# Two tiles of L1 scores move from VectorE to ScalarE and TensorE, and the scores' rows change order so that four transfers a pair spread them

## The chip, the cores and the metric

One NeuronCore of a Trainium2 chip runs the whole kernel in one launch. The metric is device time in microseconds; the other cores are idle. TensorE (matmuls into the eight PSUM banks), VectorE, ScalarE and GpSimd each run a hand-written stream of instructions, SyncE (SP) issues the transfers, and semaphores are the only order between them.

## The reference, cut to what matters

A small vision tower: a wavelet tokenizer, linear attention, a mixture of experts, then **L1-distance attention**, then a routed MLP. 128 images of 64 tokens, 64 features, 8 heads. Only the L1 attention is touched:

```python
q, vf, vb = v[:, :, :h], v[:, :, h:2*h], v[:, :, 2*h:]      # v = x @ wqv.T + b
k = x[:, :, None, :] * wk
a[b, s, t, h] = -sum_w |q[b, s, h, w] - k[b, t, h, w]| / 8   # w = 64 wide
a = softmax over s (with one extra zero row)
o = sum over heads of (a @ vf + a^T @ vb);  y = gelu-like(o) @ fanin;  x + y
```

So for every image there are 64 x 64 token pairs x 8 heads, each a sum of 64 absolute differences.

## The kernel before

Images go in pairs (`PAIRS` = 64), and the scores of each image in 16 tiles of 1024 columns. A tile is a difference q - k of 128 rows (token pairs) x 16 x 64: TensorE makes it by float16 matmuls that pick rows of q and k (high and low halves) out of `blocks`, two matmuls of 512 columns a tile. What is then done with it is set by `ORDER`, a string of 16 letters:

- **D** (11 of 16 before): VectorE reduces the absolute values straight from PSUM into `score` (`reduce`). There are two pairs of banks (0-1 and 2-3), so TensorE may be two D tiles ahead; it waits on `X["red"]` (in `image`).
- **A** (5 of 16): ScalarE takes the absolute values of banks 4 and 5, one bank at a time, into `absd` (`absolute`); GpSimd adds them up by a tree of halvings (`batch`).

The loop over pairs (`pair` on each engine) is unrolled for four pairs and then runs two pairs a turn. Between the tiles TensorE does the small work of the next and the last pairs, at positions written out by hand: in `pair` the inner function `extra(b, k)` is called after tile k of image b. Image 0 carries the next pair's turn, `queries`, `low(…, 0)` and `keys`, and the last pair's values; image 1 carries `low(…, 1)` and, for the pair before the last, `turn_attn` and the three parts of `attend`. Banks 6 and 7 serve these. `low` computes the low halves of q and k: it makes the float32 product again and takes the float16 high half from it with `neg_eye`.

When a pair's scores are complete, SP spreads them (`spread`): eight transfers an image, from 32 rows each, into `attn`, where ScalarE takes the exponentials in two parts of four heads (`exponentials`). GpSimd normalises (`normalise`). Pair q - 1's spreads and exponentials run during pair q, its attend steps during pair q + 1. SP issues, in order: `fill_blocks` for image 1, the spreads, `fill_blocks` for the next pair's image 0, and the load of a pair.

Of the kernel before, what the change touches and what calls it, by code (L numbers as in the profile page):

```python
# [36 lines left out]
ORDER = "DADDADDADDADDADD"  # L37
ND, NA = ORDER.count("D"), ORDER.count("A")
# [36 lines left out]
def constants():  # L75
# [9 lines left out]
    pick = np.zeros((4, 32, 8, 4, 32))  # L85
    for g in range(8):
        for x in range(4):
            for y in range(32):
                pick[0, 8 * x + g, g, x, y] = 1.0
                pick[1, 8 * x + g, g, x, y] = 1.0 / LO_SCALE  # L90
                pick[2, y, g, x, y] = -1.0
                pick[3, y, g, x, y] = -1.0 / LO_SCALE

    both = np.zeros((2, 32, 8, 2, 64))
    for e in range(EXPERTS):
        both[0, e, e // 2, e % 2] = 1.0
        both[1, e, e // 2, e % 2] = 1.0 / LO_SCALE
    same_head = np.kron(np.eye(16), np.ones((8, 8)))
# [5 lines left out]
        "c_both": both.reshape(64, 8 * P).astype(np.float16),  # L104
        "c_head": same_head.astype(np.float32),
# [5 lines left out]
def build(nc, a, out, scratch):  # L111

    with ExitStack() as ctx:
# [3 lines left out]
        def sem(name):  # L117
# [13 lines left out]
        c_cols = sb("c_cols_sb", [7, 2, 8, P])  # L131
# [15 lines left out]
        absd0 = sb("absd0", [P, NA * 1024])  # L147
        kT = absd0[:, 2048:3072].rearrange("p (b a m) -> p b a m", b=2, a=4)
# [35 lines left out]
        neg_eye = sb("neg_eye", [P, P], F16)  # L184
        xs1 = sb("xs1", [P, 2 * D])
# [60 lines left out]
        absd = [t[:].rearrange("p (n w) -> p n w", w=D) for t in (absd0, absd1)]  # L246
# [20 lines left out]
            "diffD", "diffA", "red", "abs", "tree", "pooled", "spread0", "spread1", "exp", "zr", "attk", "attq_ps", "attq",  # L267
# [92 lines left out]
        L1_IN = 16 * 5  # L360
        GATE = 14
        MLP_IN = 16 * 6
        PADS = 19
# [4 lines left out]
        def _(sp):  # L368
# [32 lines left out]
            sp.dma_start(rank[:], a["c_rank"]).then_inc(moe_in, 16)  # L401
            sp.dma_start(both[:].rearrange("p a b -> p (a b)"), a["c_both"]).then_inc(moe_in, 16)
# [48 lines left out]
            def pair(q, odd, at, following):  # L451
                fill_blocks(q, 1, at == 0)
                if at >= 1:
                    spread(q - 1, 1 - odd, 0, at == 1)
                    spread(q - 1, 1 - odd, 1, at == 1)
# [11 lines left out]
            spread(PAIRS - 1, 1, 0, False)  # L467
            spread(PAIRS - 1, 1, 1, False)
            sp.wait_ge(X["tb0"], 16 * 8 * (PAIRS + 1))
# [9 lines left out]
        def _(pe):  # L479
# [220 lines left out]
            def turn(p, at):  # L700

                if at >= 3:
                    pe.wait_ge(X["sum"], p - 3)
                pe.wait_ge(X["xs"], 16 * (p + 1))
                pe.transpose(ps[7][:, 0:P], xs1[:], ident[:]).then_inc(X["xT_ps"], 1)
# [43 lines left out]
            def attend(p, odd, part):  # L749

                if part == 0:
                    pe.wait_ge(X["attq"], p + 1)
# [25 lines left out]

            def image(q, b, at, extra):
# [3 lines left out]
                pe.wait_ge(X[f"tb{b}"], 16 * 8 * (q + 1))  # L783
                for k, path in enumerate(ORDER):
                    if path == "D":
                        if not (at == 0 and b == 0 and d < 2):
                            pe.wait_ge(X["red"], ND * s + d - 1)
                        unit, bank, done = 2 * d, 2 * ((b + d) % 2), "diffD"
                        d += 1
                    else:  # L790

                        for n in range(2):
                            if not (at == 0 and b == 0 and u == 0):
                                pe.wait_ge(X["abs"], 2 * NA * s + 2 * u + n - 1)
                            unit = 2 * (ND + u) + n
                            pe.matmul(ps[4 + n], pick[:, unit % 8, :], blocks[:, b, unit // 16, unit // 8 % 2, :],  # L796
                                      start=True, stop=True).then_inc(X["diffA"], 1)
# [9 lines left out]
            def pair(q, odd, at):  # L807
                def extra(b, k):
                    if b == 0:
# [16 lines left out]
                    else:  # L826
                        if k == 0:
                            low(q + 1, 1 - odd, 1)
                        if at >= 2:
                            if k == 4:  # L830
# [21 lines left out]
            fan_in(last - 2)  # L852

# [74 lines left out]
        def _(act):  # L928
            act.dma_start(c_cols[:].rearrange("p a b c -> p (a b c)"), a["c_cols"]).then_inc(tok_in, 16)
# [113 lines left out]
            def high_q(p, first):  # L1043
                act.wait_ge(X["q_ps"], p + 1)
                if not first:
                    act.wait_ge(X["tb0"], 16 * 8 * p)
                    act.wait_ge(X["tb1"], 16 * 8 * p)
# [20 lines left out]
            def absolute(s, odd, u, first):  # L1068

                for n in range(2):  # L1070
                    act.wait_ge(X["diffA"], 2 * NA * s + 2 * u + n + 1)
                    if u == 0 and n == 0 and not first:
                        act.wait_ge(X["pooled"], s - 1)
                    nc.scalar.activation(absd[odd][:, 16 * u + 8 * n:16 * u + 8 * n + 8, :],  # L1074
                                         ps[4 + n].rearrange("p (h w) -> p h w", w=D), ACT.Abs).then_inc(X["abs"], 1)

            def exponentials(p, part, first):

                if part == 0:
                    act.wait_ge(X["spread0"], 16 * 8 * (p + 1))  # L1080
# [561 lines left out]
```

## Time and profile before

| | us |
|---|---|
| median of 3 runs | 2579.07 (2578.93 to 2579.52) |
| the profiled execution | 2576.05 |
| its span, first to last instruction | 2574.2 |
| TensorE busy | 2236.6 (87%) |
| VectorE busy | 2244.8 (87%) |
| GpSimd busy | 1767.2 (69%) |
| ScalarE busy | 1475.2 (57%) |

The span is that of one execution taken by the hardware profiler. Matmuls are pipelined and their ends are modelled, so on TensorE the distance from start to start says more than the length of a record. A float32 matmul leaves two records. The L1 attention lies between about 720 and 2465 us of the span.

### The profile page before, as it was taken

What the parts mean: (1) busy time and instruction counts of PE and PEld (TensorE: products, weight loads), DVE (VectorE), ACT (ScalarE), POOL (GpSimd) and SP (SyncE); (2) the same over time, 40 slices, a digit from 0 to 9 for tenths busy, and PEclk for the clock granted to TensorE, in tenths of its full rate; (3) what the DMA queues carried; (4) which work ended last, traced back from release to release, by engine and by line L of the source; (5) the groups of instructions that cost most, each with busy time, mean ns of one, the idle gap of its engine ahead of it and who ended that gap; (6) DMA issues with size and microseconds to landing.
All of it is one profiled execution on the core that took longest, in us unless ns stands there. A gap on an engine that the chain in (4) does not pass through costs nothing.

```text
span 2574.2 us, 45353 instructions
## 1 busy us (share of the span) xinstructions
PE 2236.6 (87%) x12251; PEld 961.1 (37%) x12251; DVE 2244.8 (87%) x2638; ACT 1475.2 (57%) x3772; POOL 1767.2 (69%) x1033
## 2 busy tenths in 40 slices
PE   5558999999388989989989989899899899899878
PEld 3443333333123333333333333333333333333347
DVE  3877777777879999999999999999999999999974
ACT  0325555555146666666666666666666666666656
POOL 0112333333459889888888988888898888889843
PEclk8788999999689999999999999999999999999979
DMA  5200000000012112121211221221221212212201
GB/s 132 65 1 1 1 0 0 0 0 0 3 47 52 48 48 52 48 50 49 51 48 48 52 50 45 51 51 45 50 52 48 50 48 50 50 47 52 50 19 32
DMA packets 163216, 102.06 MB, mean 40 GB/s; under 512 B 55773, under 2 KB 161182, under 8 KB 163039
## 3 DMA queue, kind: packets, MB, share of 16 engines
q1 hardware_dynamic: 162858, 101.41, 16.0%
q8 instruction: 21, 0.34, 0.1%
q10 hardware_dynamic: 316, 0.12, 0.0%
q14 instruction: 21, 0.17, 0.0%
HBM read 10.63 MB, written 4.19 MB: 6 GB/s over the span
## 4 chain that ended last, share of the span: by engine, by line
PE 65%; DVE 23%; issue 9%; ACT 1%; DMA 1%; DVEq 0%; SPq 0%; POOL 0%; ACTq 0%; POOLq 0%
DVE score L1454 17%; PE pp L802 16%; PE pp L796 7%; PE pp L636 5%; PE pp L767 3%; PE pp L657 3%; PE pp L723 3%; PE pp L715 2%; PE pp L661 2%; PE pp L731 2%; PE pp L711 2%; PE pp L721 2%; PE pp L658 2%; PE pp L662 2%; PE pp L628 2%
## 5 line engine op out<-in xcount | busy, mean ns | idle before, releaser
L1454 DVE TENSOR_REDUCE score<-pp 128x16 f32<-128x1024 f32 x1408 | 1647.0, 1219 | 101.9 <-PE pp L802 82.2
L1571 POOL TENSOR_TENSOR absd<-absd 128x2560 f32<-128x2560 f32 x635 | 1442.4, 2271 | 197.1 <-ACT absd L1074 157.2
L802 PE MATMUL pp<-blocks,pick 128*128 128x512 f16 x2816 | 817.0, 383 | 155.0 <-DVE score L1454 150.4
L1074 ACT ACTIVATE absd<-pp 128x512 f32<-128x512 f32 x1280 | 695.4, 598 | 368.0 <-PE pp L796 364.1
L802 PEld LDWEIGHTS pp<-blocks,pick 128*128 128x128 f16 x2816 | 211.2, 98 | 590.7 <-DVE score L1454 421.9
L796 PE MATMUL pp<-blocks,pick 128*128 128x512 f16 x1280 | 400.0, 383 | 2.1
L1538 POOL TENSOR_TENSOR absd<-absd,yw 128x512 f32<-128x512 f32 x112 | 142.1, 1269 | 318.8 <-DVE yw L1376 318.8
L1008 ACT ACTIVATE absd<-pp 128x512 f32<-128x512 f32 x256 | 150.7, 596 | 148.1 <-PE pp L658 146.6
L1392 DVE SCALAR_TENSOR_TENSOR absd<-pp,absd 128x512 f32<-128x512 f32 x256 | 172.5, 688 | 52.9 <-ACT absd L1008 38.4
L796 PEld LDWEIGHTS pp<-blocks,pick 128*128 128x128 f16 x1280 | 119.8, 97 | 248.3 <-ACT absd L1074 84.6
L1056 ACT CAST qk<-pp 128x512 f16<-128x512 f32 x130 | 76.0, 585 | 191.2 <-PE pp L724 191.2
L1086 ACT ACTIVATE expd<-attn 128x65 f32<-128x65 f32 x512 | 157.5, 329 | 2.7 <-DMA attn<-score 2.7
L636 PE MATMUL pp<-absd 128*64 128x512 f32 x512 | 138.1, 618 | 0.0
L1086 ACT ACTIVATION_READ_ACCUMULATOR expd<-attn 128x1 f32 x512 | 107.6, 210 | 0.0
L657 PE MATMUL pp<-x,absd 128*128 128x512 f16 x256 | 98.4, 384 | 0.6
L661 PE MATMUL pp<-x,absd 128*128 128x512 f16 x256 | 97.8, 382 | 0.3
L658 PE MATMUL pp<-x,absd 128*128 128x512 f16 x256 | 97.5, 381 | 0.0
L662 PE MATMUL pp<-x,absd 128*128 128x512 f16 x256 | 97.4, 380 | 0.0
L1376 DVE TENSOR_TENSOR yw<-pp,absd 128x512 f32<-128x512 f32 x112 | 77.2, 689 | 17.7 <-PE pp L636 15.3
L1012 ACT COPY absd<-pp 128x512 f32<-128x512 f32 x128 | 74.9, 585 | 27.6 <-PE pp L628 18.7
L767 PEld LDWEIGHTS pp<-vb,attk 64*64 64x64 f32 x2048 | 70.7, 136 | 52.9 <-issue 52.6
L767 PE MATMUL pp<-vb,attk 64*64 64x64 f32 x2048 | 88.1, 226 | 0.0
(227 smaller groups left out, 2497.9 us busy)
## 6 DMA issues: line engine op xcount, KB each, us to landing
blocks<-qk SPq DMA_DIRECT2D x1032, 64.0 KB, 2.0
attn<-score SPq DMA_DIRECT2D x1024, 16.0 KB, 1.8
xs<-xn SPq DMA_DIRECT2D x66, 32.0 KB, 1.8
big<-in_wrb_t SPq DMA_DIRECT2D x1, 2064.0 KB
big<-in_x_rows SPq DMA_DIRECT2D x4, 512.0 KB, 6.1
token_rows<-big SPq DMA_DIRECT2D x8, 256.0 KB, 2.0
big<-in_L_ffn_w SPq DMA_DIRECT2D x4, 512.0 KB, 10.1
out<-h SPq DMA_DIRECT2D x16, 128.0 KB, 2.0
```

The source lines that it names most:

```text
L636: mm = pe.matmul(ps[4 + k % 2][64 * e:64 * e + 64, :], w3[:, 2 * k + e, :], hid[:, 2 * (k % 2) + e, :], start=True, stop=True)
L657: pe.matmul(ps[e], w12_hi[:, 0, 2 * k + e, :], x2[:, b, :], start=True, stop=False)
L661: pe.matmul(ps[2 + e], w12_hi[:, 1, 2 * k + e, :], x2[:, b, :], start=True, stop=False)
L767: mm = pe.matmul(ps[7][at, P:P + D], attk[at, n, :], vb[at, odd, n, :], start=False, stop=(n == HEADS - 1))
L796: pe.matmul(ps[4 + n], pick[:, unit % 8, :], blocks[:, b, unit // 16, unit // 8 % 2, :], start=True, stop=True).then_inc(X["diffA"], 1)
L802: mm = pe.matmul(ps[bank + n], pick[:, unit % 8 + n, :], blocks[:, b, unit // 16, unit // 8 % 2, :], start=True, stop=True)
L1008: nc.scalar.activation(silu[:, e, :], ps[e], ACT.Silu, scale=1.0 / W_SCALE).then_inc(C["silu"], 1)
L1074: nc.scalar.activation(absd[odd][:, 16 * u + 8 * n:16 * u + 8 * n + 8, :], ps[4 + n].rearrange("p (h w) -> p h w", w=D), ACT.Abs).then_inc ...
L1086: op = nc.scalar.activation(expd[:, n, :], attn[:, :, n], ACT.Exp, scale=-(float(D) ** -0.5), accum_out=zst[:, 0, n:n + 1])
L1392: dve.scalar_tensor_tensor(out=hid[:, 2 * (k % 2) + e, :], in0=ps[2 + e], scalar=1.0 / W_SCALE, in1=silu[:, e, :], op0=ALU.mult, op1=ALU.m ...
L1454: dve.tensor_reduce(score[:, odd, b, 16 * d:16 * d + 16], pp[:, bank:bank + 2, :].rearrange("p n (h w) -> p (n h) w", w=D), AX.X, ALU.add, ...
L1571: nc.gpsimd.tensor_tensor(x[:, :, 0:w], x[:, :, 0:w], x[:, :, w:2 * w], ALU.add).then_inc(X["tree"], 1)
```

## The change

`ORDER` becomes `DADDADDADDADADED`: 10 D, 5 A and one new kind of tile, E, at k = 14. For an **E** tile the operands of the matmuls are swapped (four of 256 columns): the 64 values of w now lie along the rows, and the token pairs along the columns. ScalarE takes its absolute values (`absolute` with u = 5, into `abse`). The sums over w are then TensorE's: `sum_e` multiplies the E tiles of both images by columns of ones (`pair_ones`), one quarter of the tile (two heads) after the other, each into its own 32 rows of bank 7; `copy_e` (ScalarE) brings the sums to `esum`, `turn_e` turns them with `row_of`, and `take_e` (ScalarE) writes them to the last 16 columns of `score`. All this is done for pair q - 1 during image 0 of pair q.

The constant `pick` gives the rows of a tile another order (token y outside, x inside), so that a half of an image's scores goes to `attn` by one transfer over 128 rows: four spreads a pair in place of sixteen. The first two wait for the first eight D tiles of their image only, the other two for all of them, for `pooled` and for `take_e`. The exponentials come in four parts of two heads. `low` no longer makes the float32 product again: it adds the float16 term to what stands in bank 6. `turn_attn` moves from k = 4 to k = 5, and `gated` from the reduce d = 8 to d = 7.

The diff, cut to what the prediction speaks of (the waits' constants, the constants' layout and the padding are left out):

```diff
-ORDER = "DADDADDADDADDADD"
-ND, NA = ORDER.count("D"), ORDER.count("A")
+ORDER = "DADDADDADDADADED"
+ND, NP = ORDER.count("D"), ORDER.count("A")
+NA = NP + 1
...
-    pick = np.zeros((4, 32, 8, 4, 32))
+    pick = np.zeros((4, 32, 8, 32, 4))
...
-            def spread(p, odd, b, first):
-                sp.wait_ge(X["red"], ND * (2 * p + b + 1))
-                sp.wait_ge(X["pooled"], 2 * p + b + 1)
+            def spread(p, odd, b, j, first):
+                if j == 0:
+                    sp.wait_ge(X["red"], ND * (2 * p + b) + 8)
+                else:
+                    sp.wait_ge(X["red"], ND * (2 * p + b + 1))
+                    sp.wait_ge(X["pooled"], 2 * p + b + 1)
+                    sp.wait_ge(X["etaken"], p + 1)
                 if not first:
                     sp.wait_ge(X["exp"], p)
-                for j in range(2):
-                    for x in range(4):
-                        sp.dma_start(attn[64 * b + 32 * j:64 * b + 32 * j + 32, 16 * x:16 * x + 16, :].rearrange("p s h -> p (s h)"),
-                                     score[32 * x:32 * x + 32, odd, b, P * j:P * j + P]).then_inc(X[f"spread{b}"], 16)
+                sp.dma_start(attn[64 * b + 32 * j:64 * b + 32 * j + 32, 0:S, :].rearrange("p s h -> p (s h)"),
+                             score[:, odd, b, P * j:P * j + P]).then_inc(X[f"spread{b}"], 16)
...
             def low(p, odd, kind):
                 pe.wait_ge(X["half"], 4 * p + 2 * kind + 1)
-                if kind:
-                    pe.matmul(ps[6], xT1[:, odd, :], wk_diag[:].rearrange("p h d -> p (h d)"), start=True, stop=False)
-                else:
-                    pe.matmul(ps[6], xTq[:], wqv[:, 0:QK], start=True, stop=False)
-                pe.matmul(ps[6], neg_eye[:], qk[:, kind, 0, :], start=False, stop=True).then_inc(X["klo_ps" if kind else "qlo_ps"], 1)
+                pe.matmul(ps[6], neg_eye[:], qk[:, kind, 0, :], start=False, stop=True, skip_group_check=True).then_inc(X["klo_ps" if kind else "qlo_ps"], 1)
...
+            def sum_e(p, first):
+                pe.wait_ge(X["abs"], 4 * NA * (p + 1))
+                if not first:
+                    pe.wait_ge(X["etaken"], p)
+                for m in range(4):
+                    for b in range(2):
+                        mm = pe.matmul(ps[7][32 * m:32 * m + 32, 0:2 * P], pair_ones[:, b, :], abse[b][:, m, :],
+                                       start=(b == 0), stop=(b == 1))
+                mm.then_inc(X["e_ps"], 1)
+
+            def turn_e(p):
+                pe.wait_ge(X["esum"], p + 1)
+                for g in range(2):
+                    mm = pe.matmul(ps[7][:, 256 + 16 * g:272 + 16 * g], esum[:, P * g:P * g + P], row_of[:], start=True, stop=True)
+                mm.then_inc(X["et_ps"], 1)
...
                         for n in range(2):
                             if not (at == 0 and b == 0 and u == 0):
                                 pe.wait_ge(X["abs"], 2 * NA * s + 2 * u + n - 1)
...
+                            else:
+                                for m in range(2):
+                                    mm = pe.matmul(ps[4 + n][:, 256 * m:256 * m + 256],
+                                                   blocks[:, b, 1, 1, P * (2 * n + m):P * (2 * n + m) + P],
+                                                   pick[:, 6:8, :].rearrange("p a b -> p (a b)"), start=True, stop=True)
...
+                        if k == 11 and at >= 1:
+                            sum_e(q - 1, at == 1)
+                        if k == 13 and at >= 1:
+                            turn_e(q - 1)
...
+            def copy_e(p):
+                act.wait_ge(X["e_ps"], p + 1)
+                act.wait_ge(X["et_ps"], p)
+                nc.scalar.copy(esum[:], ps[7][:, 0:2 * P]).then_inc(X["esum"], 1)
+
+            def take_e(p, odd, at):
+                act.wait_ge(X["et_ps"], p + 1)
...
+                nc.scalar.copy(score[:, odd, :, 240:256].rearrange("p b (g h) -> p g b h", g=2),
+                               ps[7][:, 256:288].rearrange("p (g b h) -> p g b h", g=2, b=2)).then_inc(X["etaken"], 1)
```

How the streams move, at the three places that matter. First TensorE at the end of image 0 (from k = 10's `queries` on), in the unrolled pairs. The rows name line, operation, output and inputs, shape and how many. Before (L711 queries, L802 D tiles, L723 and L724 low, L796 an A tile, L715 keys):

```order
L711 MATMUL pp<-wqv,xTq 128x512
L802 MATMUL pp<-blocks,pick 128x512 x4
L723 MATMUL pp<-wqv,xTq 128x512
L724 MATMUL pp<-qk,neg_eye 128x512
L796 MATMUL pp<-blocks,pick 128x512 x2
L802 MATMUL pp<-blocks,pick 128x512 x2
L715 MATMUL pp<-wk_diag,xT 128x512
L802 MATMUL pp<-blocks,pick 128x512 x4
```

And now (L735 queries, L850 D tiles, L810 sum_e, L838 an A tile, L744 low, L817 turn_e, L842 the E tile, L739 keys):

```order
L735 MATMUL pp<-wqv,xTq 128x512
L850 MATMUL pp<-blocks,pick 128x512 x2
L810 MATMUL pp<-absd,pair_ones 32x256 x8
L838 MATMUL pp<-blocks,pick 128x512 x2
L744 MATMUL pp<-qk,neg_eye 128x512
L850 MATMUL pp<-blocks,pick 128x512 x2
L817 MATMUL pp<-row_of,esum 128x16 x2
L842 MATMUL pp<-pick,blocks 128x256 x4
L739 MATMUL pp<-wk_diag,xT 128x512
L850 MATMUL pp<-blocks,pick 128x512 x4
```

Between `queries` and `keys` there were three D tiles and are two now; `sum_e`, `turn_e` and the E tile are new among them, and the float32 part of `low` is gone.

Second, TensorE at the end of image 1, from the last part of `attend` (L767) to the next pair's values (L731). Before:

```order
L767 MATMUL pp<-vb,attk 64x64 x8
L796 MATMUL pp<-blocks,pick 128x512 x2
L802 MATMUL pp<-blocks,pick 128x512 x4
L796 MATMUL pp<-blocks,pick 128x512 x2
L802 MATMUL pp<-blocks,pick 128x512 x6
L731 MATMUL pp<-wqv,xT 128x512
```

And now (L789 is attend, L751 the values):

```order
L789 MATMUL pp<-vb,attk 64x64 x8
L838 MATMUL pp<-blocks,pick 128x512 x2
L850 MATMUL pp<-blocks,pick 128x512 x2
L838 MATMUL pp<-blocks,pick 128x512 x2
L850 MATMUL pp<-blocks,pick 128x512 x2
L842 MATMUL pp<-pick,blocks 128x256 x4
L850 MATMUL pp<-blocks,pick 128x512 x4
L751 MATMUL pp<-wqv,xT 128x512
```

The tiles for ScalarE now alternate with D tiles one by one.

Third, ScalarE over the same end of image 1. Before (L1074 absolutes, L1097 the gate, L1086 exponentials, L1062 the next pair's values):

```order
L1097 ACTIVATE osb<-pp 128x64
L1086 ACTIVATE expd,zst<-attn 128x65 x4
L1074 ACTIVATE absd<-pp 128x512 x2
L1086 ACTIVATE expd,zst<-attn 128x65 x4
L1074 ACTIVATE absd<-pp 128x512 x2
L1062 COPY vb<-pp 128x512
```

And now (L1133 absolutes of A, L1136 of E, L1174 the gate, L1163 exponentials, L1118 the values):

```order
L1174 ACTIVATE osb<-pp 128x64
L1163 ACTIVATE expd,zst<-attn 128x65 x2
L1133 ACTIVATE absd<-pp 128x512 x2
L1163 ACTIVATE expd,zst<-attn 128x65 x2
L1136 ACTIVATE absd<-pp 128x512 x2
L1163 ACTIVATE expd,zst<-attn 128x65 x2
L1133 ACTIVATE absd<-pp 128x512 x2
L1118 COPY vb<-pp 128x512
```

Two of the eight exponentials have gone ahead of this piece (behind the A tile of k = 7), and E's absolutes stand between the last two parts.

## Rows read from the trace of the kernel before

**Rows 1.** The page: busy times, the chain by engine, VectorE's costliest group.

```profile
PE 2236.6 (87%) x12251; PEld 961.1 (37%) x12251; DVE 2244.8 (87%) x2638; ACT 1475.2 (57%) x3772; POOL 1767.2 (69%) x1033
...
PE 65%; DVE 23%; issue 9%; ACT 1%; DMA 1%; DVEq 0%; SPq 0%; POOL 0%; ACTq 0%; POOLq 0%
...
L1454 DVE TENSOR_REDUCE score<-pp 128x16 f32<-128x1024 f32 x1408 | 1647.0, 1219 | 101.9 <-PE pp L802 82.2
```

**Rows 2.** Timeline of VectorE: start, length, line, operation, [idle before].

```profile
1507.16 2.36 DVE L1454 TENSOR_REDUCE score<-pp 128x16 f32<-128x1024 f32 x2 [0.36 <-PE pp L802]
...
1513.31 3.49 DVE L1454 TENSOR_REDUCE score<-pp 128x16 f32<-128x1024 f32 x3 [0.16 <-PE pp L802]
...
1516.86 3.49 DVE L1454 TENSOR_REDUCE score<-pp 128x16 f32<-128x1024 f32 x3
1520.51 2.36 DVE L1454 TENSOR_REDUCE score<-pp 128x16 f32<-128x1024 f32 x2 [0.16 <-PE pp L802]
1523.11 10.88 DVE L1454 TENSOR_REDUCE score<-pp 128x16 f32<-128x1024 f32 x9 [0.24 <-PE pp L802]
1534.35 2.36 DVE L1454 TENSOR_REDUCE score<-pp 128x16 f32<-128x1024 f32 x2 [0.36 <-PE pp L802]
```

**Rows 3.** Timeline of TensorE, end of image 0.

```profile
1518.14 0.60 PE L802 MATMUL pp<-blocks,pick 128*128 128x512 f16 x2 [0.35 <-DVE score L1454]
...
1519.02 1.02 PE L711 MATMUL pp<-wqv,xTq 96*128 96x512 f32 x2
1519.88 1.13 PE L802 MATMUL pp<-blocks,pick 128*128 128x512 f16 x4
1520.86 1.13 PE L723 MATMUL pp<-wqv,xTq 96*128 96x512 f32 x2
...
1522.05 0.59 PE L796 MATMUL pp<-blocks,pick 128*128 128x512 f16 x2
...
1522.91 1.10 PE L715 MATMUL pp<-wk_diag,xT 96*128 96x512 f32 x2
1523.84 0.60 PE L802 MATMUL pp<-blocks,pick 128*128 128x512 f16 x2
```

**Rows 4.** Timeline of ScalarE, ends of both images.

```profile
1522.24 0.58 ACT L1056 CAST qk<-pp 128x512 f16<-128x512 f32 x1 [1.43 <-PE pp L724]
1522.72 1.09 ACT L1074 ACTIVATE absd<-pp 128x512 f32<-128x512 f32 x2
...
1533.70 1.08 ACT L1074 ACTIVATE absd<-pp 128x512 f32<-128x512 f32 x2 [2.37 <-PE pp L796]
...
1534.77 0.34 ACT L1086 ACTIVATE expd<-attn 128x65 f32<-128x65 f32 x1
...
1535.08 0.33 ACT L1086 ACTIVATE expd<-attn 128x65 f32<-128x65 f32 x1
```

**Rows 5.** Timeline of GpSimd: a batch, and the normalising.

```profile
1509.95 11.68 POOL L1571 TENSOR_TENSOR absd<-absd 128x2560 f32<-128x2560 f32 x5 [1.08 <-ACT absd L1074]
...
1521.99 1.04 POOL L1582 TENSOR_TENSOR attk<-expd,zst 128x512 f32<-128x512 f32 x1
```

**Rows 6.** Timeline of TensorE: values_f, and the tile behind it.

```profile
1515.20 1.08 PE L738 MATMUL pp<-wqv,xT 96*64 96x256 f32 x8
1516.22 0.60 PE L802 MATMUL pp<-blocks,pick 128*128 128x512 f16 x2
```

**Rows 7.** Timeline of TensorE from 1515.15 to 1515.25: values_f alone.

```profile
1515.20 0.44 PE L738 MATMUL pp<-wqv,xT 96*64 96x256 f32 x2
```

**Rows 8.** Timeline of TensorE: tiles among the attend steps.

```profile
1529.83 0.59 PE L796 MATMUL pp<-blocks,pick 128*128 128x512 f16 x2
...
1532.12 0.61 PE L802 MATMUL pp<-blocks,pick 128*128 128x512 f16 x2
...
1533.71 1.03 PE L802 MATMUL pp<-blocks,pick 128*128 128x512 f16 x4
```

**Rows 9.** The page's transfers: KB each, us from issue to landing.

```profile
attn<-score SPq DMA_DIRECT2D x1024, 16.0 KB, 1.8
```

More of the change, by code:

```diff
@@ L97, in constants @@
         both[1, e, e // 2, e % 2] = 1.0 / LO_SCALE
+    row_of = np.zeros((4, 32, 2, 4, 2))
+    for m in range(4):
+        for b in range(2):
+            for a in range(2):
+                row_of[m, 2 * b + a, b, m, a] = 1.0
     same_head = np.kron(np.eye(16), np.ones((8, 8)))
@@ L453, in pair @@
                 if at >= 1:
-                    spread(q - 1, 1 - odd, 0, at == 1)
-                    spread(q - 1, 1 - odd, 1, at == 1)
+                    for j in range(2):
+                        for b in range(2):
+                            spread(q - 1, 1 - odd, b, j, at == 1)
                 fill_blocks(q + 1, 0, False)
@@ L466, in _ @@
                     pair(2 * i + odd, odd, 4, bass.ds(2 * i + odd + 2, 1))
-            spread(PAIRS - 1, 1, 0, False)
-            spread(PAIRS - 1, 1, 1, False)
-            sp.wait_ge(X["tb0"], 16 * 8 * (PAIRS + 1))
+            for j in range(2):
+                for b in range(2):
+                    spread(PAIRS - 1, 1, b, j, False)
+            sp.wait_ge(X["tb0"], FILL * (PAIRS + 1))
             sp.wait_ge(X["xs"], 16 * (PAIRS + 2))
@@ L852, in _ @@
             fan_in(last - 2)
+            pe.wait_ge(X["sum"], last - 1)
+            sum_e(last, False)
+            turn_e(last)
+            pe.wait_ge(X["etaken"], PAIRS)
             def last_turn(p):
@@ L1110, in pair @@
                     turned_y(q - 3)
-                absolute(s, 0, 1, first)
+                absolute(s, 0, 1, q, first)
                 if at >= 1:
                     values_f(q - 1, 1 - odd)
-                absolute(s, 0, 2, first)
+                absolute(s, 0, 2, q, first)
                 prepare_x(q + 1, 1 - odd)
-                absolute(s, 0, 3, first)
+                absolute(s, 0, 3, q, first)
                 high_q(q + 1, False)
+                if at >= 1:
+                    copy_e(q - 1)
+                absolute(s, 0, 4, q, first)
                 low(q + 1, 0)
-                absolute(s, 0, 4, first)
+                if at >= 1:
+                    take_e(q - 1, 1 - odd, at - 1)
+                absolute(s, 0, 5, q, first)
                 s += 1
@@ L1131, in pair @@
                 if at >= 1:
-                    exponentials(q - 1, 0, at == 1)
-                absolute(s, 1, 4, first)
+                    exponentials(q - 1, 1, at == 1)
+                absolute(s, 1, 4, q, first)
                 if at >= 1:
-                    exponentials(q - 1, 1, at == 1)
+                    exponentials(q - 1, 2, at == 1)
+                absolute(s, 1, 5, q, first)
+                if at >= 1:
+                    exponentials(q - 1, 3, at == 1)
             act.wait_ge(pads, PADS)
@@ L1151, in _ @@
             values_f(last, 1)
+            copy_e(last)
+            take_e(last, 1, 4)
             def root(c):
@@ L1175, in _ @@
             turned_y(last - 1)
-            exponentials(last, 0, False)
-            exponentials(last, 1, False)
+            for part in range(4):
+                exponentials(last, part, False)
             root(0)
@@ L1206, in _ @@
                 dve.memset(t, 0.0).then_inc(pads, 1)
-            dve.wait_ge(pads, 14)
+            dve.wait_ge(pads, 15)
             for t in (xT4[D:D + 1, :], xT1[D:D + 1], xTq[D:D + 1, :], yT[D:D + 1, :], xT5[D:D + 1]):
                 dve.memset(t, 1.0).then_inc(pads, 1)
+            for half in range(2):
+                at = slice(64 * half, 64 * half + 64)
+                for b in range(2):
+                    dve.memset(pair_ones[at, b, 2 * b + half:2 * b + half + 1], 1.0)
             dve.memset(wk_bd[:], 0.0)
```

102 lines of the change are left out of this document (64 added, 38 removed).

## The prediction

> **What bounds the kernel now.** I read the page first: its busy row and the chain [rows 1]. VectorE and TensorE are both at 87% of the span, and the chain that ended last runs over TensorE for 65% and VectorE for 23%. So neither alone is the bound; what counts is how the two hand tiles to each other. The stretch that the change touches is the L1 attention, 64 pairs of images. VectorE's timeline there [rows 2] repeats: the group of two that starts at 1507.16 with 0.36 idle ahead of it starts again at 1534.35, so a pair takes 27.18 us.
>
> VectorE's free-running pace comes from a group of three reduces: 3.49 us for three [rows 2], with one alone at 1.22 [rows 1], so (3.49 - 1.22) / 2 = 1.13 us a reduce. 22 of them are 24.9 us; the three small operations between them add about 0.6; the other 1.7 of the 27.18 us are gaps, put on TensorE's tiles: 0.16, 0.24 and 0.36 are shown as such, and the nine reduces from 1523.11 take 10.88 where 8 x 1.13 + 1.22 is 10.26. TensorE may be only two D tiles ahead (two pairs of banks), so any stretch in which TensorE has more than 1.13 us of work per D tile becomes idle time of VectorE, however idle TensorE is elsewhere.
>
> TensorE's prices, from start to start [rows 3]: a tile 0.44 (1518.14 to 1519.02 holds two); a float32 matmul of 512 columns 0.86 (1519.02 to 1519.88); the old low step, a float32 and a float16 one, 1.19 (1520.86 to 1522.05); keys with the wait into it 0.93 (1522.91 to 1523.84). A tile's reduce starts 0.63 after its first matmul (1519.88 to 1520.51), and TensorE reuses a bank 0.15 after a reduce ends (1516.86 + 1.13 = 17.99, matmul at 18.14).
>
> **The change on the path.** One D tile an image goes: 2 x 1.13 = 2.26 us less VectorE work a pair. ScalarE gets four more absolutes (0.48 each: a pair of them takes 1.08 with one at 0.60 [rows 4]), about 2.0 us, and two small copies; it is 57% busy, so throughput is no concern, its latency is. GpSimd needs 2 x 12.04 + 1.04 = 25.1 us a pair [rows 5]; that is the floor below which the period cannot go, and it starts earlier now (it waits for five A tiles, the last at k=12). SP's sixteen spread issues become four; they lie beside other work before and after.
>
> The cost is on TensorE. New there: sum_e, eight float32 matmuls of 256 columns into 32-row groups, and turn_e. The trace has no 32-wide one. The nearest is values_f [rows 6]: four float32 matmuls of 256 columns, alternating between two halves of the array, take 1.02 from start to start, 0.16 of it change-over; so two run beside each other, and one alone is 0.43. In sum_e the two matmuls of a quarter follow each other on the same columns (image 0, image 1), and only the last of a quarter can run beside the first of the next if they start in program order: five steps of 0.43 = 2.15, with the change-over 2.3 us. Bounds: all four quarters beside each other, 0.86 + 0.16 = 1.0; nothing beside anything, 3.44 + 0.16 = 3.6. I take 2.3, because values_f shows overlap only between neighbours in the program, and nothing in between the bounds has a row.
>
> The page "TensorE: Matmul & The Clock Gate" of the Trainium skill (section "The mechanism") has matmuls start and end in strict program order, which by this count also gives 2.15. The page "TensorEngine Tiling (Array Packing)" (sections "Theoretical Speedup" and "Key Properties") says that 32-wide tiles work independently, up to 4 times as fast, which would give the lower bound; the trace shows two at once [rows 6] and cannot say which page holds for this order.
>
> Image 0's end, walked on the clock of the pair shown [rows 2, 3] (the leading 15 of a time is left out), unchanged up to D at k=11 (19.88, its reduce 20.51 to 21.64). sum_e 20.31 to 22.61. A (k=12) to 23.05, the low step now only its float16 half (0.22) to 23.26, D (k=13) 23.26, its reduce at 23.89: VectorE idle for 2.25. Then turn_e, about 0.35 (two loads and 16 columns, like the small steps), E 24.05 to 24.5. keys waits for ScalarE: copy_e, absolutes of k=12 at 23.08 and 23.56, the cast of low from 24.05 (0.58 [rows 4]) to 24.63, keys 24.7 to 25.66, D (k=15) 25.66, its reduce at 26.29. The reduce before it ended at 25.02: 1.27 idle. Image 1's first reduce comes at 27.42. From there VectorE is fed at its own pace (low is 0.97 shorter too) until the attend steps: A at 31.40, and by [rows 8] 2.29 from there to the second tile behind it and 1.59 to the third, so the D at k=11 is issued at 35.28 and reduced at 35.91 instead of 34.35 [rows 2]: **1.56 us later**.
>
> Image 1's end. Before, D at k=11 and 12 are fed together. Now A at k=12 and E at k=14 are only one D apart, and each waits for ScalarE's buffer. ScalarE, shifted back to the old clock: two absolutes and the gate 33.70 to 34.77, two exponentials (0.31 each) to 35.38, absolutes of k=12 35.38 and 35.86, free at 36.0 and 36.5 [rows 4]. So E's second half starts at 36.53, D (k=15) at 36.75, its reduce at 37.38 where it could have been 36.82: 0.56 idle. The next pair's first reduce is at 38.51, its second at 39.83, where it was at 40.49 (1513.31 [rows 2] plus the period): **0.66 earlier**, of the 1.13 that the missing reduce would give.
>
> Sum: 1.56 - 0.66 = +0.90 us a pair. 63 pairs run with sum_e beside them: +56.7. Pair 0 has no sum_e and gains about 2; at the end four transfers replace sixteen (about -3) but TensorE has sum_e and turn_e ahead of the last turns (about +3). The sum is +54.7: the profiled execution took 2576.05 (span 2574.2), so 2630.8; on the median 2579.07, 3.0 above it, 2633.8. I say 2634 us, 2.1% slower.
>
> **Waits added.** On TensorE turn_e waits for copy_e; behind it stand E, keys and D (k=15), for which VectorE waits. copy_e is ready at about 23.1, turn_e is wanted at 23.7: free. On ScalarE copy_e waits for sum_e, and behind it stand the absolutes of k=12, which start no earlier anyway. take_e stands ahead of E's absolutes and high_k: 0.1. On SP the second two spreads wait for take_e (24.7) and land by 28 (two issues, and 1.8 to landing [rows 9]); the first exponentials, now one A tile ahead of where they stood, want them after that tile's absolutes at 33: 5 us of cover. fill_blocks for the next image 0 is issued as before after image 0's last D, with all of image 1 as its cover. None of them costs.
>
> **The rivals.**
> 1. *Quarters beside each other* (faster). If the four 32-wide groups run independently in spite of their order, sum_e costs 1.0, 1.3 less each pair: 0.90 - 1.29 = -0.39, or -25 us: 2552. For it: a float32 matmul leaves two records, 0.21 apart when alone, and in values_f's first 0.05 us two records start and end within 0.44 [rows 7]: they can only be of the two halves, so the second half's first pass starts ahead of the first half's second. If the passes are queued one by one, that is already an overtaking. Against it: if a matmul is queued whole, it is none, and no row shows a whole matmul overtake a waiting one. It decides at sum_e = 1.4 us: below that the kernel is faster. This is also the tiling page's rule of the Trainium skill. Chance 0.36.
> 2. *No overlap at all*: sum_e 3.6, 2714. values_f speaks against it. 0.03.
> 3. *ScalarE's buffers do not hold E up* at image 1's end: 0.56 less a pair, -35: 2599. My walk there leans on half a dozen latencies. 0.09.
> 4. *The full effect*: the gaps close and the period falls to GpSimd's floor with its hand-overs, 25.4: -1.8 x 63 = -113, 2467. It needs 3.5 us of gaps to vanish. 0.03.
> 5. *The forecast*, 2.3 us of sum_e and the waits as walked: its own range 2608 to 2660 (0.4 us a pair either way). 0.42. The remaining 0.07 are other costs, a late transfer or a slower 32-wide load.
>
> **How the numbers follow.** Range 2545 to 2672: it takes in the forecast, rivals 1 and 3, and leaves out 2, 4, half of the rest and the edge of 1, about 0.15. No change means within 0.2% (5 us), about what three runs can tell here. Faster: rival 1 nearly whole, rival 4, some of the rest: 0.39. Same: where 1 and 3 err towards each other, 0.05. Slower: the forecast, 2, 3 and half of the rest: 0.56.
>
> **What the changed profile would show.** sum_e's group of sixteen records: about 2.3 us long (2.15 and the tail) if right, about 1.1 in rival 1, over 3.4 in rival 2. VectorE's timeline: 20 reduces a pair; idle of about 2.2 before the D after sum_e and of about 1.3 before the last D of image 0, put on TensorE; 0.5 before the last of image 1 with TensorE waiting for ScalarE there. The period 28.1 us, against 26.8 in rival 1 and 25.4 in rival 4. GpSimd's idle should grow, and no transfer should end a wait. The forecast is wrong if sum_e is short, or if VectorE's gaps stand elsewhere.

## The result, and the profile after: 2540.3 us, 1.5% faster where 2.1% slower was forecast

| | us |
|---|---|
| before | 2579.07 (2578.93 to 2579.52) |
| after | 2540.32 (2539.4 to 2541.42) |
| ratio, 95% interval | 0.985 (0.9833 to 0.9867) |
| span of the profiled execution, before and after | 2574.2 and 2539.3 |

The forecast's sign was wrong, and the time lies below its range (2545 to 2672). It is the side of rival 1, and some 12 us beyond that rival's own number.

The page after, with its busy row, the chain by engine and VectorE's group (as [rows 1]):

```profile
PE 2232.0 (88%) x13527; PEld 999.4 (39%) x13527; DVE 2096.2 (83%) x2515; ACT 1634.4 (64%) x4156; POOL 1765.2 (70%) x1033
...
PE 52%; DVE 24%; issue 12%; ACT 9%; DMA 1%; DVEq 1%; ACTq 0%; POOL 0%; SPq 0%; POOLq 0%
...
L1548 DVE TENSOR_REDUCE score<-pp 128x16 f32<-128x1024 f32 x1280 | 1498.8, 1217 | 214.2 <-PE pp L850 212.8
```

VectorE lost 148 us of reduces and 112 of them came back as idle time ahead of them, 214.2 where it was 101.9. VectorE's timeline of a pair shows where:

```profile
1493.69 2.36 DVE L1548 TENSOR_REDUCE score<-pp 128x16 f32<-128x1024 f32 x2 [0.47 <-PE pp L850]
...
1499.55 3.48 DVE L1548 TENSOR_REDUCE score<-pp 128x16 f32<-128x1024 f32 x3
1503.19 1.23 DVE L1548 TENSOR_REDUCE score<-pp 128x16 f32<-128x1024 f32 x1 [0.16 <-PE pp L850]
1505.40 1.22 DVE L1548 TENSOR_REDUCE score<-pp 128x16 f32<-128x1024 f32 x1 [0.98 <-PE pp L850]
1507.76 9.28 DVE L1548 TENSOR_REDUCE score<-pp 128x16 f32<-128x1024 f32 x8 [1.14 <-PE pp L850]
1517.39 1.23 DVE L1548 TENSOR_REDUCE score<-pp 128x16 f32<-128x1024 f32 x1 [0.36 <-PE pp L850]
...
1520.44 2.36 DVE L1548 TENSOR_REDUCE score<-pp 128x16 f32<-128x1024 f32 x2 [0.47 <-PE pp L850]
```

The two groups with 0.47 ahead of them are one pair apart, 26.75 us (the pairs alternate, 26.79 on the mean), against 27.18 in [rows 2]. The three new gaps stand where the forecast put them. Behind sum_e it is 0.98 and not 2.25; ahead of image 0's last D 1.14 (forecast 1.27), ahead of image 1's last 0.47 (0.56). A group of columns is, below, the part of TensorE's array that a matmul uses (32, 64 or all 128 columns); it gives the rows of the bank to which the matmul writes. TensorE's timeline shows what made the first gap small (L810 is sum_e, L817 turn_e, L842 the E tile, L739 keys):

```profile
1502.56 0.59 PE L850 MATMUL pp<-blocks,pick 128*128 128x512 f16 x2
1503.08 1.09 PE L810 MATMUL pp<-absd,pair_ones 128*32 128x256 f32 x16
1504.11 0.60 PE L838 MATMUL pp<-blocks,pick 128*128 128x512 f16 x2
1504.55 0.38 PE L744 MATMUL pp<-qk,neg_eye 128*128 128x512 f16 x1
1504.77 0.59 PE L850 MATMUL pp<-blocks,pick 128*128 128x512 f16 x2
1505.20 0.52 PE L817 MATMUL pp<-row_of,esum 128*128 128x16 f32 x4
1505.56 0.60 PE L842 MATMUL pp<-pick,blocks 128*128 128x256 f16 x4
1506.16 1.13 PE L739 MATMUL pp<-wk_diag,xT 96*128 96x512 f32 x2
```

sum_e takes 1.03 us from start to start (1503.08 to 1504.11), the lower bound of the forecast to 0.01. The same timeline over 1503.05 to 1503.3 alone holds four of its records, all begun and ended within 0.44:

```profile
1503.08 0.44 PE L810 MATMUL pp<-absd,pair_ones 128*32 128x256 f32 x4
```

One float32 matmul's two records stand 0.2 us apart, so these are the first passes of four matmuls on four groups of columns, though each quarter's second matmul stands in the program ahead of the next quarter's first.

**The account.** The trace's view by line of the stage's reciprocals (start of the first and of the last at the end of the list of times), before:

```profile
L1439 DVE RECIPROCAL zst<-zst x64: 191/193/203, 775.6 to 2482.6; 128x8 f32<-128x8 f32 x64
```

And after:

```profile
L1533 DVE RECIPROCAL zst<-zst x64: 190/192/204, 772.7 to 2446.7; 128x8 f32<-128x8 f32 x64
```

Between them lie 1707.0 and 1674.0 us: 33.0 of the 34.9 that the spans differ by. 63 pairs x 0.40 are 25.2. Another 6.5 goes with TensorE's clock. In the kernel before it falls four times in the stage; this is each engine's busy time over these stretches, with the granted clock third from the end:

```profile
882.20:885.60 3.40, 3.40 (x7) 1.36 (x7) 2.23 (x3) 0.42 (x3) 3.40 (x1) 0.50 0.39 94
1264.50:1267.90 3.40, 3.40 (x7) 1.32 (x8) 2.33 (x3) 0.37 (x3) 3.40 (x1) 0.50 0.38 93
1674.10:1677.50 3.40, 3.40 (x7) 1.33 (x6) 2.21 (x3) 0.42 (x3) 3.40 (x1) 0.50 0.39 95
2056.40:2059.80 3.40, 3.40 (x7) 1.32 (x8) 2.31 (x3) 0.36 (x3) 3.40 (x1) 0.50 0.38 93
```

0.50 is 1.2 GHz. The four pairs in which they lie took 28.8 us where the others took 27.19: 1.6 us each, 6.5 together. All four begin at the same place of a pair, the end of image 1, about 2 us ahead of the reciprocals, where TensorE waits for VectorE to free banks. The 3 us ahead of the first fall, and the same stretch of a pair after the change (its reciprocals start at 879.7):

```profile
879.20:882.20 3.00, 1.42 (x6) 0.34 (x6) 3.00 (x5) 3.00 (x17) 1.72 (x3) 1.00 0.00 0
```

```profile
874.60:877.60 3.00, 2.42 (x12) 0.90 (x12) 2.53 (x4) 3.00 (x14) 1.33 (x2) 1.00 0.01 3
```

TensorE was busy for 1.42 of these 3 us before and is busy for 2.42 now. The other pairs before had the same 1.42 without a fall, so this alone does not set one off. After the change the stage has none:

```profile
725.00:1300.00 575.00, 525.29 (x3316) 224.45 (x3313) 508.31 (x490) 424.83 (x1136) 518.05 (x274) 1.00 0.20 50
1300.00:1900.00 600.00, 552.64 (x3589) 240.01 (x3589) 529.55 (x517) 444.69 (x1218) 543.90 (x292) 1.00 0.20 50
1900.00:2440.00 540.00, 495.00 (x3250) 216.24 (x3250) 474.90 (x460) 396.44 (x1080) 483.50 (x264) 1.00 0.20 50
```

TensorE is busy for 91 to 92% of these stretches (against 1549 us of the 1715 between 725 and 2440 before, 90%). The rest is the two ends: the first reciprocal comes 2.9 us earlier, the last pairs give 1.3 and the code behind the last reciprocal takes 1.0 more. 2.9 + 25.2 + 6.5 + 1.3 - 1.0 = 34.9.

### The profile page after: what moved, and what is told of

Same layout as the page of the kernel before. It is cut to its first block, busy times and chain, and to the rows that moved or that the text cites. A ratio compares the mean times of both kernels' runs of the same rounds, so it can differ in the third digit from the quotient of the medians.

```text
span 2539.3 us, 48447 instructions
## 1 busy us (share of the span) xinstructions
PE 2232.0 (88%) x13527; PEld 999.4 (39%) x13527; DVE 2096.2 (83%) x2515; ACT 1634.4 (64%) x4156; POOL 1765.2 (70%) x1033
## 4 chain that ended last, share of the span: by engine, by line
PE 52%; DVE 24%; issue 12%; ACT 9%; DMA 1%; DVEq 1%; ACTq 0%; POOL 0%; SPq 0%; POOLq 0%
DVE score L1548 19%; PE pp L850 10%; ACT absd L1133 6%; PE pp L658 5%; PE pp L838 4%; PE pp L789 3%; PE pp L739 3%; PE pp L810 3%; PE pp L679 3%; PE pp L683 2%; PE pp L735 2%; PE pp L684 2%; PE pp L680 2%; PE pp L650 2%; PE pp L784 2%
## 5 line engine op out<-in xcount | busy, mean ns | idle before, releaser
L1548 DVE TENSOR_REDUCE score<-pp 128x16 f32<-128x1024 f32 x1280 | 1498.8, 1217 | 214.2 <-PE pp L850 212.8
L1133 ACT ACTIVATE absd<-pp 128x512 f32<-128x512 f32 x1280 | 696.0, 598 | 274.2 <-PE pp L838 274.1
L850 PE MATMUL pp<-blocks,pick 128*128 128x512 f16 x2560 | 750.5, 382 | 100.8 <-DVE score L1548 82.1
L838 PE MATMUL pp<-blocks,pick 128*128 128x512 f16 x1280 | 394.8, 382 | 9.3 <-ACT absd L1133 0.5
L850 PEld LDWEIGHTS pp<-blocks,pick 128*128 128x128 f16 x2560 | 196.7, 98 | 467.3 <-DVE score L1548 312.9
L1064 ACT ACTIVATE absd<-pp 128x512 f32<-128x512 f32 x256 | 150.8, 596 | 148.1 <-PE pp L680 145.7
L838 PEld LDWEIGHTS pp<-blocks,pick 128*128 128x128 f16 x1280 | 114.7, 97 | 207.1 <-ACT absd L1133 59.8
L1163 ACT ACTIVATE expd<-attn 128x65 f32<-128x65 f32 x512 | 162.9, 337 | 0.0
L1136 ACT ACTIVATE absd<-pp 128x512 f32<-128x512 f32 x256 | 143.9, 638 | 0.0
L842 PE MATMUL pp<-pick,blocks 128*128 128x256 f16 x512 | 88.6, 274 | 29.8 <-ACT absd L1133 23.7
L1163 ACT ACTIVATION_READ_ACCUMULATOR expd<-attn 128x1 f32 x512 | 111.5, 218 | 0.0
```

What stands on the lines that cost most here:

```text
L838: mm = pe.matmul(ps[4 + n], pick[:, unit % 8, :], blocks[:, b, unit // 16, unit // 8 % 2, :], start=True, stop=True)
L850: mm = pe.matmul(ps[bank + n], pick[:, unit % 8 + n, :], blocks[:, b, unit // 16, unit // 8 % 2, :], start=True, stop=True)
L1064: nc.scalar.activation(silu[:, e, :], ps[e], ACT.Silu, scale=1.0 / W_SCALE).then_inc(C["silu"], 1)
L1163: op = nc.scalar.activation(expd[:, n, :], attn[:, :, n], ACT.Exp, scale=-(float(D) ** -0.5), accum_out=zst[:, 0, n:n + 1])
L1548: dve.tensor_reduce(score[:, odd, b, 16 * d:16 * d + 16], pp[:, bank:bank + 2, :].rearrange("p n (h w) -> p (n h) w", w=D), AX.X, ALU.add, ...
```

## The experiments

The theory after the result: the time follows sum_e's length one for one, the sign with it, and TensorE starts a matmul as soon as its own columns are free. Rivals: the gain has another source in the change; or the overtaking has a limit.

### sums_128_wide: no two of the sums beside each other

```diff
-                        mm = pe.matmul(ps[7][32 * m:32 * m + 32, 0:2 * P], pair_ones[:, b, :], abse[b][:, m, :],
-                                       start=(b == 0), stop=(b == 1))
+                        mm = pe.matmul(ps[7][:, 0:2 * P], pair_ones[:, b, 96 - 32 * m:224 - 32 * m], abse[b][:, m, :],
+                                       start=(m == 0 and b == 0), stop=(m == 3 and b == 1))
```

(`pair_ones` is 224 wide, with its ones at column 96.)

> Base is the changed kernel (2540.3 us, sum_e 1.03 us from start to start, period 26.79 us a pair). Here each of sum_e's eight matmuls is 128 columns wide, so none can run beside another: 8 x 0.43 + 0.16 = 3.6 us. Theory (the sign hangs on sum_e's length, and it stands on the path one for one): 2.57 us more a pair, x 63 = +162, 2702 us, slower than before by 4.8%. Rival (the length matters little, since TensorE has slack, and the gain has another source): under 2600 us.

Measured 2690.44 us, ratio to before 1.043 (1.0413 to 1.0448). sum_e from start to start, in TensorE's timeline:

```profile
1509.52 3.62 PE L810 MATMUL pp<-absd,pair_ones 128*128 128x256 f32 x16
1512.97 0.59 PE L838 MATMUL pp<-blocks,pick 128*128 128x512 f16 x2
```

The gap behind it, in VectorE's:

```profile
1514.25 1.23 DVE L1548 TENSOR_REDUCE score<-pp 128x16 f32<-128x1024 f32 x1 [3.31 <-PE pp L850]
```

3.45 us, 2.42 more than in the changed kernel, and the gap grows from 0.98 to 3.31, by 2.33; 150 us in all are 2.38 a pair. The length of sum_e is paid one for one. I had expected 3.6 and 2702 us: 8 x 0.43 is 3.44 already, so between matmuls that all use the full width the change-over of 0.16 does not appear, which is 0.15 x 63 = 9.5 of the 12 us. Between 2540.3 and 2690.4 the kernel crosses 2579.1 at 1.03 + 2.42 x 38.8 / 150.1 = 1.66 us of sum_e.

### sums_64_wide: what may overtake

```diff
-                        mm = pe.matmul(ps[7][32 * m:32 * m + 32, 0:2 * P], pair_ones[:, b, :], abse[b][:, m, :],
-                                       start=(b == 0), stop=(b == 1))
+                        mm = pe.matmul(ps[7][64 * (m // 2):64 * (m // 2) + 64, 0:2 * P],
+                                       pair_ones[:, b, 32 - 32 * (m % 2):96 - 32 * (m % 2)], abse[b][:, m, :],
+                                       start=(m % 2 == 0 and b == 0), stop=(m % 2 == 1 and b == 1))
```

> Base is the changed kernel. sum_e's matmuls are 64 columns wide, four on the lower half of the columns and then four on the upper half, in this order in the program. Theory A (a matmul waits only for its own columns, those behind it on other columns start at once): the halves run beside each other, 4 x 0.43 + 0.16 = 1.9 us, 0.86 more a pair, +54, 2594 us. Theory B (only one matmul can be set aside for each group of columns, the next one stops the queue): the upper half starts 0.86 late, sum_e 2.7, +107, 2647 us. Theory C, of the forecast (strict program order): 7 x 0.43 + 0.16 = 3.2, +137, 2677 us.

Measured 2649.9 us (1.0274, 1.0257 to 1.0292): theory B. TensorE's timeline, the whole of sum_e:

```profile
1520.26 2.86 PE L810 MATMUL pp<-absd,pair_ones 128*64 128x256 f32 x16
1523.06 0.61 PE L839 MATMUL pp<-blocks,pick 128*128 128x512 f16 x2
```

Its beginning, in the same timeline cut off at 1521.15:

```profile
1520.26 1.08 PE L810 MATMUL pp<-absd,pair_ones 128*64 128x256 f32 x4
```

And cut off at 1521.25:

```profile
1520.26 1.35 PE L810 MATMUL pp<-absd,pair_ones 128*64 128x256 f32 x6
```

Until 1521.15 only four records have begun, one after the other (two matmuls on the lower half); between 1521.15 and 1521.25 two begin together. So the upper half's first matmul starts when the lower half's third does, having overtaken only the fourth; it does not start at once (theory A: 1.9 us) and it does not wait for all four (theory C: 3.2). Which record belongs to which half is read from these starts; the trace does not name the columns. sum_e is 2.80. What holds the third matmul back is open: in this trace the weight loads keep the same order as the matmuls, the upper half's first one starting at 1521.18 with its matmul, and no run separates the two.

### sums_64_pairs: the same matmuls, two on each half in turn

(The diff is against sums_64_wide.)

```diff
-                for m in range(4):
+                for m in (0, 2, 1, 3):
```

> As sums_64_wide (2649.9 us, sum_e 2.7 us), with the program's order two matmuls on the lower half, two on the upper, and again. Theory B (for each group of columns one matmul runs and one is set aside; a third stops the queue): nothing stops for long, the halves run beside each other, sum_e 4 x 0.43 + 0.16 = 1.9 us, 0.86 above the changed kernel, +54, 2594 us. If the width were the cause and not the order: 2650 us again.

Measured 2593.92 us (1.0056, 1.0039 to 1.0073), 56 us below sums_64_wide by the order alone. TensorE's timeline:

```profile
1525.54 2.00 PE L810 MATMUL pp<-absd,pair_ones 128*64 128x256 f32 x16
1527.47 0.60 PE L839 MATMUL pp<-blocks,pick 128*128 128x512 f16 x2
```

1.93 us. The rule holds for the two halves: on each one float32 matmul runs and one is set aside, and those on the other pass it; a third for the same half stops the queue. On 32 columns the changed kernel shows the passing, and no run here puts a third matmul behind them.

### sums_alternate: image 0's sums for all quarters, then image 1's

```diff
-                for m in range(4):
-                    for b in range(2):
+                for b in range(2):
+                    for m in range(4):
```

> The changed kernel with sum_e's eight matmuls in the order image 0 for all quarters, then image 1 for all quarters. Theory B (one matmul runs and one is set aside for each group of columns, others start at once): sum_e 1.03 as before, 2540 us. If the order mattered to 32-wide matmuls at all: a time outside 2535 to 2545.

Measured 2535.87 us (0.9835, 0.982 to 0.985), inside the band, with a sum_e of 1.00 us: the order is nearly free. It is 4.5 us below the changed kernel. Of this 2.3 us lie between the first and the last reciprocal (1671.7 against 1674.0); 2.6 lie ahead of the first, where the two kernels do the same work, and are not the order's.

### before_low_only: the part of the change that pays

The kernel before with this alone:

```diff
-                if kind:
-                    pe.matmul(ps[6], xT1[:, odd, :], wk_diag[:].rearrange("p h d -> p (h d)"), start=True, stop=False)
-                else:
-                    pe.matmul(ps[6], xTq[:], wqv[:, 0:QK], start=True, stop=False)
-                pe.matmul(ps[6], neg_eye[:], qk[:, kind, 0, :], start=False, stop=True).then_inc(
+                pe.matmul(ps[6], neg_eye[:], qk[:, kind, 0, :], start=False, stop=True, skip_group_check=True).then_inc(
```

> The kernel before, with only low's float32 product left out (11 D and 5 A tiles, sixteen transfers as before). Theory (most of the gain is low's; the E tile alone costs what it saves): in image 0's end and image 1's start the kernel before has gaps of 0.33, 0.24 and 0.22 us a pair behind the two long low steps; they close, 0.75 us a pair x 64 = -48, 2531 us, about the changed kernel's time. Rival (the E tile carries the gain and low helps only to pay for it): 2560 us or more.

Measured 2528.04 us (0.9802, 0.9785 to 0.9818): 12 us **faster than the whole change**; the theory had 2531, about as fast. VectorE's timeline at image 0's end (to be read beside [rows 2], 1520.51 and 1523.11):

```profile
1521.04 11.52 DVE L1450 TENSOR_REDUCE score<-pp 128x16 f32<-128x1024 f32 x10 [0.16 <-PE pp L798]
```

Ten reduces almost without a gap: 9 x 1.13 + 1.22 = 11.4. A pair takes 26.38 us by the profile, 0.81 less than before. Its clock falls six times in the stage, for 3.4 us each; three stretches, before, in and behind one:

```profile
1030.00:1033.00 3.00, 1.58 (x6) 0.30 (x5) 3.00 (x4) 3.00 (x18) 1.49 (x3) 1.00 0.00 1
1033.40:1036.80 3.40, 3.40 (x8) 1.46 (x7) 2.08 (x3) 0.58 (x2) 3.40 (x1) 0.50 0.39 96
1037.00:1040.00 3.00, 2.82 (x18) 1.21 (x16) 2.67 (x3) 2.03 (x5) 2.92 (x2) 1.00 0.31 75
```

TensorE was busy for 1.58 of the first 3 us shown; all six falls begin, as before, at the end of image 1. The rest of the change adds 0.41 us a pair to this (26.79), 26 us over 63 pairs, and gives back about 10 because no fall comes with it and 2 in the last pair: 13.8 us between the first and the last reciprocal (1674.0 against 1660.2). The rest is the E tile with its sums and waits, the exponentials in four parts, the moved `turn_attn` and `gated`, and the rows' order with its transfers. Only the last was tried by itself (before_four_transfers); that the 0.41 is the E tile's is argued from the gap behind sum_e.

### low_with_product: the changed kernel without that part

The same edit the other way round.

> Base is the changed kernel, with low's float32 product made again as before the change. By the walk along image 0's end, 0.97 us stand between sum_e and the D tile of k=13, for which VectorE waits already, and another 0.97 at the start of image 1, where two tiles of lead hide most: 1.1 to 1.3 us more a pair, +70 to +83, 2610 to 2623 us, slower than before. Rival (TensorE hides it, ScalarE sets keys' start): under 2560 us.

Measured 2589.73 us (1.0041, 1.0027 to 1.0056): on the expected side, two thirds of the size. Without low's shortening, the rest of the change is slower than the kernel before. VectorE's timeline behind image 0's last quarter:

```profile
1502.39 1.23 DVE L1552 TENSOR_REDUCE score<-pp 128x16 f32<-128x1024 f32 x1 [1.84 <-PE pp L854]
1504.48 2.35 DVE L1552 TENSOR_REDUCE score<-pp 128x16 f32<-128x1024 f32 x2 [0.87 <-PE pp L854]
```

The gap behind sum_e grows by 0.86 (0.98 to 1.84); the one ahead of image 0's last D shrinks by 0.27 (1.14 to 0.87), which my expectation had left out.

### before_four_transfers: the rows' order and the spreads alone

```diff
-                for j in range(2):
-                    for x in range(4):
-                        sp.dma_start(attn[64 * b + 32 * j:64 * b + 32 * j + 32, 16 * x:16 * x + 16, :].rearrange("p s h -> p (s h)"),
-                                     score[32 * x:32 * x + 32, odd, b, P * j:P * j + P]).then_inc(X[f"spread{b}"], 16)
+                for j in range(2):
+                    sp.dma_start(attn[64 * b + 32 * j:64 * b + 32 * j + 32, 0:S, :].rearrange("p s h -> p (s h)"),
+                                 score[:, odd, b, P * j:P * j + P]).then_inc(X[f"spread{b}"], 16)
```

(With `pick` in the new order.)

> The kernel before, with only the rows' order and the spreads changed (two transfers of 128 rows an image in place of eight of 32; their waits are those of before). Theory (the transfers lie beside other work, SP is never waited for): the period stays 27.19, at the end of the stage some 3 us are saved, 2574 to 2579 us. Rival (sixteen issues delay fill_blocks): under 2560 us.

Measured 2577.67 us (0.9993, 0.9983 to 1.0002): no difference that can be measured. The pair takes 27.19 us as before. By the profiles the last pair is 2.4 us shorter, near the 3 expected, and the stage has five falls of the clock where the kernel before has four, which takes 1.6 of it back. The transfers lie beside other work; their earlier start and the new waits of the changed kernel are not in this run.

### before_low_keys_late: is the E tile worth its place?

before_low_only with keys moved behind k=0 of image 1 (the edit of keys_late, below).

> The kernel before, with low's product left out and keys moved to image 1, and no E tile: what the E tile is worth once TensorE's load is levelled. VectorE needs 22 x 1.13 + 0.6 = 25.5 us and keeps about 0.6 of gaps (0.25 behind queries, 0.45 behind attend): 26.1 to 26.3 us a pair, 2510 to 2522 us. If the E tile is worth its place, this is slower than keys_late (2474.0 us, 25.79 us a pair); if not, it equals it.

Measured 2535.08 us (0.9827, 0.9811 to 0.9844), 26.63 us a pair: 13 to 25 us above what I expected, and 7 above before_low_only, where image 0's end had no gap left to close. There keys only moves TensorE's work into image 1. It is 61 us slower than keys_late, so with keys late the E tile, with what came with it, is worth its place.

### keys_late: TensorE's load levelled between the images

```diff
-                        if k == 14:
-                            keys(q + 1, 1 - odd)
                     else:
                         if k == 0:
+                            keys(q + 1, 1 - odd)
+                        if k == 2:
                             low(q + 1, 1 - odd, 1)
...
                 high_k(q + 1)
-                low(q + 1, 1)
                 absolute(s, 1, 0, q, first)
+                low(q + 1, 1)
```

> Base is the changed kernel, with keys moved from behind k=14 of image 0 to behind k=0 of image 1, and low of k behind k=2. Theory (VectorE's gap of 1.14 us ahead of image 0's last D is keys and its wait for ScalarE, and TensorE has slack in image 1): period 26.8 to about 25.9, -0.9 x 64 = -58, 2482 us. Rival (GpSimd's floor of about 25.4 or ScalarE's absolutes take over, or the gap moves into image 1): 2500 to 2540 us.

Measured 2473.99 us (0.9593, 0.9577 to 0.9609), 4.1% faster than before and 8 us below the theory's 2482. VectorE's timeline from the D behind sum_e on, into image 1:

```profile
1526.11 10.67 DVE L1548 TENSOR_REDUCE score<-pp 128x16 f32<-128x1024 f32 x9 [0.98 <-PE pp L850]
1537.13 1.23 DVE L1548 TENSOR_REDUCE score<-pp 128x16 f32<-128x1024 f32 x1 [0.36 <-PE pp L850]
```

The gap of 1.14 is gone into a run of nine reduces, 0.4 longer than nine reduces without gaps; 25.79 us a pair.

### keys_late_exp_later: ScalarE's order at image 1's end

(The diff is against keys_late.)

```diff
-                if at >= 1:
-                    exponentials(q - 1, 1, at == 1)
                 absolute(s, 1, 4, q, first)
                 if at >= 1:
-                    exponentials(q - 1, 2, at == 1)
+                    exponentials(q - 1, 1, at == 1)
                 absolute(s, 1, 5, q, first)
                 if at >= 1:
+                    exponentials(q - 1, 2, at == 1)
                     exponentials(q - 1, 3, at == 1)
```

> keys_late (2474.0 us, 25.78 us a pair), with ScalarE's order at image 1's end changed: the second part of the exponentials behind the absolutes of k=12, the third and fourth behind those of E. Theory (TensorE waits for ScalarE's buffers at k=12 and k=14, as forecast, and VectorE's gaps of 0.22 and 0.56 us there come from this): they shrink to about 0.1 together, but GpSimd needs 25.1 us a pair and waits only about 1.2 us a pair in keys_late: 25.2 to 25.5 us a pair, 2438 to 2458 us. Rival (the exponentials end too late for the reciprocals, which VectorE does behind the next pair's first reduce, or GpSimd's floor is reached): 2465 to 2480 us.

Measured 2460.81 us (0.9542, 0.9529 to 0.9555), the best version, 4.6% faster than before. It is 3 us above the theory's band (2438 to 2458) and 4 below the rival's (2465 to 2480). VectorE's timeline at a pair's end:

```profile
1507.69 3.48 DVE L1547 TENSOR_REDUCE score<-pp 128x16 f32<-128x1024 f32 x3
1511.09 0.19 DVE L1532 RECIPROCAL zst<-zst 128x8 f32<-128x8 f32 x1
1511.45 3.48 DVE L1547 TENSOR_REDUCE score<-pp 128x16 f32<-128x1024 f32 x3 [0.16 <-PE pp L850]
```

GpSimd's, where batches of absolute values alternate with the attention's products:

```profile
1507.94 11.67 POOL L1664 TENSOR_TENSOR absd<-absd 128x2560 f32<-128x2560 f32 x5
...
1519.98 1.04 POOL L1675 TENSOR_TENSOR attk<-expd,zst 128x512 f32<-128x512 f32 x1
1521.17 8.62 POOL L1664 TENSOR_TENSOR absd<-absd 128x2560 f32<-128x2560 f32 x2 [0.15 <-ACT absd L1133]
```

The last two D tiles of image 1 and the next pair's first are reduced in one run, so the gap of 0.47 was ScalarE's buffers; 0.25 of it is gained. A pair takes 25.54 us, and GpSimd, which needs 25.1, now idles for 0.15 ahead of a batch: the next bound is near.

## Why the prediction was wrong, by its own steps

- **The step that failed** is "only the last of a quarter can run beside the first of the next if they start in program order: five steps of 0.43 = 2.15". sum_e takes 1.03. Each quarter's second matmul is set aside and the next quarter's first passes it (sums_64_wide and sums_64_pairs show on two halves that one, and only one, is set aside). The page "TensorE: Matmul & The Clock Gate" of the Trainium skill (section "The mechanism"), with its strict program order, does not hold for these float32 matmuls: 1.03 us, where that order gives 2.3. The page "TensorEngine Tiling (Array Packing)" of the Trainium skill (section "Key Properties") gives this case's length, but not that of sums_64_wide, where tiles that work independently would have given 1.9 and 2.8 was measured.
- Part of the evidence stood in [rows 7], the records of two halves starting together, and rival 1 got 0.36 for it. "No row shows a whole matmul overtake a waiting one" was true, and was no reason to prefer the other end.
- **The price a pair.** Rival 1's -0.39 was measured as -0.40. The two other new gaps were right to 0.13: the walk along the streams held, only its first term did not. "It decides at sum_e = 1.4" came out at 1.66; most of the difference is the terms in the next point.
- **The 12 us beyond rival 1** are 6.5 that go with four falls of TensorE's clock, which I had not looked for in this stage (the 64 us slices of the profile's page round them away), 0.6 from the price a pair, and 1.2 from the two ends (3.2 where the forecast had 2). The other 3.8 are between the profiled executions, 35.0 us apart, and the medians, 38.8 apart. None of these was in rival 1's sum; without them the time would lie inside the range, on rival 1's number.
- **Which part gains** the forecast did not ask. Its sum ran over both, and "the low step now only its float16 half" carried everything: alone it gives 0.81 us a pair, and the rest of the change, the E tile with sum_e, turn_e and its wait above all, costs 0.41 of it again.
- **The waits added** cost nothing that the trace shows, as said: from 900 to 2300 us no engine sits idle ahead of turn_e or of an exponential. keys waits for ScalarE for 0.3 us a pair, about as walked. The transfers gain nothing (before_four_transfers).

## What to carry to other kernels

Where two engines hand tiles over with a lead of two, walk the stretch in which the feeder's extra work is densest, and move that work to where the feeder waits: keys moved by two tiles was worth 66 us, more than the whole change. Where no gap stands, the same move gains nothing: on before_low_only it cost 7 us. When a change bundles a cheap deletion with an expensive reshaping, price each alone: here the deletion alone beat the bundle. When two bounds of an unmeasured cost lie on the two sides of no change, the chances should say so more evenly than a preferred mechanism suggests.

## What the runs showed of the hardware that was not expected

- Float32 matmuls on 32 or 64 columns of the array pass one waiting matmul of another group of columns. On 64 columns they stop at the second one waiting for the same group (not tried on 32). Eight of them, streaming 256 columns each, take 1.03 us on four groups, 1.93 on two in pairs, 2.80 on two in fours, 3.45 on all columns.
- TensorE's clock fell to 1.2 GHz for 3.4 us at a time inside a stage in which it was busy for 90%, four times before the change, six times in before_low_only, in which it had less to do, once in before_low_keys_late, and not at all in the changed kernel. Each cost 1.6 us. All began at the same place, where TensorE had been busy for 1.4 to 1.5 of the last 3 us, though the same stretch of most pairs had no fall. What exactly sets it off was not tried.
